# Adjacency words turned by a DMA instead of packed on TensorE, and VectorE's sorted rows begun three chunks later in layer 1

## The reference

```
h = relu(layernorm(x));  Wh = h @ W
e = Wh @ a[:256] + (Wh @ a[256:]).T          # layer 0: no nonlinearity on e
x = x + leaky_relu(softmax(where(adj, e, -1e9)) @ Wh, 0.2)
h = relu(layernorm(x))
e = leaky_relu(h @ a1[:256] + (h @ a1[256:]).T, 0.01)
x = x + softmax(where(adj, e, -9e15)) @ h    # layer 1
```

## Time and profile before

| | us |
|---|---|
| runs | 1846.00, 1840.76, 1846.56 |
| profiled execution | 1844.22 |
| its span | 1842.1 |
| PE busy | 1701.4 (92%) |
| DVE busy | 1224.0 (66%) |
| ACT busy | 940.5 (51%) |
| POOL busy | 650.3 (35%) |
| layer 0, first to last aggregate after the start | 155.12 to 1139.8 |
| POOL orders the lists | 901.45 to 1096.2 |
| first layer 1 gather to the last's start | 1148.59 to 1815.58 |

### The profile page before, as it was taken

One profiled execution on the slowest core, in us unless ns is written; L12 is line 12 of the kernel. 1 busy time (PEld: TensorE's weight loads), 2 busy tenths in 40 slices (PEclk: granted clock), 3 DMA queues, 4 the chain that ended last, 5 costly groups with the idle time before them and its releaser, 6 DMA issues. The chain is left out here.

```text
span 1842.1 us, 46596 instructions
## 1 busy us (share of the span) xinstructions
PE 1701.4 (92%) x17795; PEld 1460.9 (79%) x17795; DVE 1224.0 (66%) x4738; ACT 940.5 (51%) x1303; POOL 650.3 (35%) x607
## 2 busy tenths in 40 slices
PE   6889999999999999999999997677689999899887
PEld 5648888888888888888888886555578888788776
DVE  6577887888888888875533333677655655555655
ACT  5976554644565555546555541755444444444432
POOL 0000000000000000000255540888877777777775
PEclk9999999999999999999999999888989999999999
DMA  8409877978887797879999981644544444354442
GB/s 301 163 27 383 306 258 272 336 278 298 306 302 274 297 337 270 299 286 357 325 355 361 359 272 53 163 129 134 152 108 128 112 133 107 107 140 112 124 111 86
DMA packets 144110, 410.88 MB, mean 223 GB/s; under 512 B 26193, under 2 KB 92626, under 8 KB 111186
## 3 DMA queue, kind: packets, MB, share of 16 engines
q1 hardware_dynamic: 109714, 329.85, 49.8%
q0 software_dynamic: 27904, 73.43, 14.3%
q10 hardware_dynamic: 6336, 5.77, 1.1%
HBM read 368.94 MB, written 40.03 MB: 222 GB/s over the span
## 5 line engine op out<-in xcount | busy, mean ns | idle before, releaser
L956 PE MATMUL banks<-HV,adjT 128*128 128x257 f16 x8192 | 938.0, 273 | 5.6 <-DVE HV L656 5.2
L956 PEld LDWEIGHTS banks<-HV,adjT 128*128 128x128 fp8e4 x8192 | 788.7, 97 | 138.7 <-DVE HV L656 22.3
L1609 PE MATMUL banks<-Vp,adjp 128*128 128x257 f16 x2560 | 502.3, 278 | 92.7 <-DVE Vn L1409 53.4
L1235 POOL DMA_INDIRECT gat<-h_of_layer,rec x420 | 479.6, 1142 | 127.8 <-issue 125.7
L1609 PE MATMUL banks<-Vn,adjn 128*128 128x257 f16 x2560 | 501.4, 278 | 0.0
L428 ACT ACTIVATE adj_f<-adj_i 128x2048 fp8e4<-128x2048 int32 x256 | 474.1, 1897 | 6.8 <-DMA adj_i<-in_adj 4.5
L1609 PEld LDWEIGHTS banks<-Vp,adjp 128*128 128x128 fp8e4 x2560 | 249.9, 99 | 142.2 <-DVE Vn L1409 57.1
L409 POOL DMA_DIRECT2D HV<-x_after_layer x44 | 25.6, 581 | 849.6 <-DVE rank L879 796.6
L1609 PEld LDWEIGHTS banks<-Vn,adjn 128*128 128x128 fp8e4 x2560 | 252.6, 99 | 41.6
L1271 ACT ACTIVATE adjn<-h1bc,nh 128x512 fp8e5<-128x512 f32 x320 | 208.5, 711 | 104.0 <-PE banks L1609 93.4
L493 ACT ACTIVATE std<-mv,eps 128x1 f32<-128x1 f32 x64 | 18.8, 294 | 306.8 <-DVE mv L688 306.7
(11 more groups left out here) (157 smaller groups left out, 1455.5 us busy)
## 6 DMA issues: line engine op xcount, KB each, us to landing
adj_i<-in_adj SPq DMA_DIRECT2D x256, 1024.0 KB, 7.8
h_of_layer<-hh SPq DMA_DIRECT2D x64, 129.0 KB, 6.0
hs<-h_of_layer SPq DMA_DIRECT2D x64, 129.0 KB, 2.6
xt<-in_x SPq DMA_DIRECT2D x64, 128.0 KB, 6.1
packed_adj<-pk SPq DMA_DIRECT2D x64, 128.0 KB, 6.4
x_after_layer<-x SPq DMA_DIRECT2D x64, 128.0 KB, 6.0
HV<-in_x SPq DMA_DIRECT2D x7, 1024.0 KB, 11.9
gat<-h_of_layer,rec POOLq DMA_INDIRECT x420
```

The lines of the kernel that those rows point to most:

```text
L956: last = nc.tensor.matmul(acc[b][:, 0:DV], adjT_h[:, b, jb, :], V0[:, jb, s, 0:DV], start=(jb == 0 and s == 0), stop=(jb == T - 1 and s == 1))
L1235: pool.indirect_dma_start(gat[:, k % NBUF, s - s0, :], None, h_d, bass.IndirectOffsetOnAxis(ap=rec[:, m, s:s + 1], axis=0))\
L1609: mm = nc.tensor.matmul(bank[2 * i + part][:, 0:DV], m[:, i * P:(i + 1) * P], V[:, j, s, 0:DV], start=(j == 0 and s == 0), stop=(j == T - ...
```

## The change

It has three parts.

**The words are made on DVE and turned by a DMA.** `pack`, its constant and its PSUM banks are gone, and DVE's cast with them. The words are now those of `fold` (made for all 64 tiles); `turn`, an instruction on ACT's queue, transposes the 128x512 words in four 128x128 blocks into `pk` and signals `word_in`. `unpack` on DVE waits for that. Since the folded words pair other columns than the packed ones, tile and row numbers are permuted: a pair of tiles holds rows two apart (`x_v`, `adj_v`, `out_v`), `place` gives the bit and byte of a block, and PE's weights are read from `adjT` with a stride of two bytes, in layer 1 too.

**The steps are ordered anew.** ACT converts tile t+3 in step t (before: t+2) and turns t+2 at its end. DVE does fold part 0 of t+2, extract of t+1, unpack of t+1, decode, finish of t-1 with the other folds of t+2. `decode_bits` moves from the last of four steps to the third. SP's order is not touched.

**Layer 1.** Unpack is four operations of 128x512 for two chunks instead of eight of 128x256. With HEAD = 3.0, `rows_by` becomes 0, 0, 0, 0, 5, 12, 19, 26, 33, 40 and still ends at 420 after chunk 79.

The core of the diff:

```diff
+    def place(t):
+
+        k, q = divmod(t // 2, BQ)
+        return q, (k & 1) * 4 + (k & 2) + k // 4, t % 2
...
-    x_v = x.rearrange("(t p) d -> p t d", p=P)
-    adj_v = adj.rearrange("(t p) n -> t p n", p=P)
-    out_v = out.rearrange("(t p) d -> p t d", p=P)
+    x_v = x.rearrange("(m p h) d -> p m h d", p=P, h=2)
+    adj_v = adj.rearrange("(m p h) n -> m h p n", p=P, h=2)
+    out_v = out.rearrange("(m p h) d -> p m h d", p=P, h=2)
...
+                def turn(t, b, pb, reuse):
+
+                    act.wait_ge(fold_ready, t * 3 + 3)
+                    if reuse is not None:
+                        act.wait_ge(pk_out[pb], reuse)
+                    act.sem_inc(quarters_seen, 1)
+                    act.dma_start_transpose(pk[:, pb, :].rearrange("p (q r) -> p q r", q=BQ),
+                                            fold1[:, b, 1, :].bitcast(u16)).then_inc(word_in[pb], 16)
...
+                def step(t, j, reuse, pk_reuse, converts=True, turns=True):
+
+                    if converts:
+                        convert(t + 3, (j + 1) % 2, range(0, Q // 2), False)
+                    copy_sums(t - 1, (j - 1) % 2)
+                    if converts:
+                        convert(t + 3, (j + 1) % 2, range(Q // 2, Q), False)
+                    if reuse is not None:
+                        act.wait_ge(hh_out[(j - 1) % NX], reuse)
+                    finish(t - 1, (j - 1) % NX)
+                    if turns:
+                        turn(t + 2, j % 2, (j + 2) % NPK, pk_reuse)
```

```diff
-                    sp.wait_ge(pk_ready, t + 1)
-                    sp.dma_start(pk_d[bass.ds(t + off, 1), :, :].rearrange("o p n -> p (o n)"),
-                                 pk[:, pb, :]).then_inc(pk_out[pb], 16)
+                    sp.wait_ge(word_in[pb], 16 * (t // NPK + 1))
+                    sp.dma_start(pk_d[t + off, :, :], pk[:, pb, :]).then_inc(pk_out[pb], 16)
...
+                def unpack(t, b, pb, n_in):
+
+                    dve.wait_ge(word_in[pb], n_in)
+                    for i in range(HALF):
+                        if i <= 6:
+                            last = nc.vector.tensor_scalar(adjT[:, b, i, :], pk[:, pb, :], PAIR << i, 6 - i,
+                                                           ALU.bitwise_and, ALU.logical_shift_left)
                         else:
-                            i = nc.vector.tensor_scalar(dst, words, PAIR << k, k - 6, ALU.bitwise_and,
-                                                        ALU.logical_shift_right)
-                    i.then_inc(adjT_ready, 1)
+                            last = nc.vector.tensor_scalar(adjT[:, b, i, :], pk[:, pb, :], PAIR << i, i - 6,
+                                                           ALU.bitwise_and, ALU.logical_shift_right)
+                    last.then_inc(adjT_ready, 1)
...
-                def step(t, j, pk_reuse, n_in, x1_reuse, kept, off, ahead=True, lists=False, taken=False, e=None):
-
-                    if n_in is not None:
-                        normalise(t - 1, (j - 1) % 2)
+                def step(t, j, n_in, x1_reuse, kept, off, word_n, ahead=True, folds=True, listed=False,
+                         taken=False, e=None):
+
+                    normalise(t - 1, (j - 1) % 2)
+                    if folds:
+                        fold(t + 2, j % 2, 0)
+                    if taken:
+                        extract(t + 1, (j + 1) % UN)
                     if ahead:
-                        take_packed(t + 1, (j + 1) % 2, (j + 1) % NPK, pk_reuse, lists)
-                    if taken:
-                        extract(t, j % UN)
+                        unpack(t + 1, (j + 1) % 2, (j + 1) % NPK, word_n)
                     if e is not None:
-                        decode(e, (j + 1) % UN)
-                    if n_in is not None:
-                        finish(t - 1, (j - 1) % NX, n_in, x1_reuse, kept, off,
-                               (t + 1, (j + 1) % 2) if lists else None)
+                        decode(e, (j + 2) % UN)
+                    finish(t - 1, (j - 1) % NX, n_in, x1_reuse, kept, off,
+                           (t + 2, j % 2) if folds else None, listed)
...
-                        pack(k * 2 + b + 1, (b + 1) % 2, False)
                         aggregate(k * 2 + b, b)
```

```diff
-                            last = nc.tensor.matmul(acc[b][:, 0:DV], adjT_h[:, b, jb, :],
+                            q, i, h = place(jb)
+                            last = nc.tensor.matmul(acc[b][:, 0:DV], adjT_h[:, b, i, q, :, h],
...
+        HEAD = 3.0
...
-        pace = [FIRST * min(n, NC) + max(0, n - NC) for n in range(C)]
+        pace = [max(0.0, FIRST * min(n, NC) + max(0, n - NC) - HEAD) for n in range(C)]
...
-                    words = pkg[:, c // (NC // 2), :, :].rearrange("p g (t w) -> p t g w", w=WPB)
-                    for k in range(HALF):
-                        dst = adjp[:, c // UB % 2, :, :].rearrange("p t (g i) -> p t g i", g=G)\
-                            [:, :, :, k * WPB:(k + 1) * WPB]
-                        src = words[:, c % (NC // 2) * CB:(c % (NC // 2) + UB) * CB, :, :]
-                        if k <= 6:
-                            i = nc.vector.tensor_scalar(dst, src, PAIR << k, 6 - k, ALU.bitwise_and,
-                                                        ALU.logical_shift_left)
+                    q = c * CB // BITS % (BQ // 2)
+                    words = pkg[:, c // (NC // 2), :, q * P:(q + 1) * P]
+                    for k in range(UB * CB // 2):
+                        i = c * CB % BITS // 2 + k
+                        dst = adjp[:, c // UB % 2, k, :].rearrange("p (g r) -> p g r", g=G)
+                        if i <= 6:
+                            made = nc.vector.tensor_scalar(dst, words, PAIR << i, 6 - i, ALU.bitwise_and,
+                                                           ALU.logical_shift_left)
```

More of the change, by code:

```diff
@@ L634, in _ @@
                 for t in range(T - TAKE, T - TAKE + XC - 2):
                     take_wh(t)
-                    if t in UNPACKS:
-                        take_packed(UNPACKS[t], UNPACKS[t], UNPACKS[t], None)
+                    if t in FOLDS:
+                        for part in range(4):
+                            fold(FOLDS[t], FOLDS[t], part)
                 scales(NCH - 1)
@@ L646, in _ @@
                 nc.vector.memset(fl[:, :], 0.0)
+                unpack(0, 0, 0, 16)
+                unpack(1, 1, 1, 16)
                 dve.wait_ge(M_ready, 1)
@@ L699, in finish @@
                         fold(*folds, 3)
-                        fold(*folds, 4)
+                    if listed:
+                        make_keys(*folds)
                     dve.wait_ge(hh_ready, t + 1)
@@ L882, in _ @@
                 dve.wait_ge(v0_ready, T)
-                dve.wait_ge(const_in, 16 * 6)
+                dve.wait_ge(const_in, 16 * 5)
                 for t in range(2):
-                    fold(t, t, 0)
-                for t in range(2):
-                    for part in range(1, 5):
-                        fold(t, t, part)
-                    if t == 0:
-                        extract(0, 0)
+                    make_keys(t, t)
+                    extract(t, t)
+                for part in range(4):
+                    fold(2, 0, part)
+                make_keys(2, 0)
                 dve.wait_ge(hh_ones, 1)
                 for t in range(1, 2 * UN):
-                    step(t, t % UN, *counts(t), lists=True, taken=True,
-                         e=(t + 1) // UN - 1 if t >= UN - 1 else None)
+                    step(t, t % UN, *counts(t), listed=True, taken=True, e=(t - 2) // UN if t >= 2 else None)
                 with dve.Fori(2, NS // UN - 1) as k:
@@ L897, in _ @@
                 for t in range(NS - UN, T):
-                    step(t, t % UN, *counts(t), ahead=t + 1 < T, lists=t + 1 < NS,
-                         taken=t < NS, e=(t + 1) // UN - 1 if t < NS + UN - 1 else None)
+                    step(t, t % UN, *counts(t), ahead=t + 1 < T, folds=t + 2 < T, listed=t + 2 < NS,
+                         taken=t + 1 < NS, e=(t - 2) // UN if t < NS + 2 else None)
                     if t == SORT:
@@ L913, in _ @@
                 pe.wait_ge(ucol_ready, 2)
-                def pack(t, b, first):
-                    if not first:
-                        pe.wait_ge(pk_ready, t - 1)
-                    for q in range(Q):
-                        pe.wait_ge(conv_done, t * Q + q + 1)
-                        pe.sem_inc(quarters_due, 1)
-                        for jb in range(q * QB, (q + 1) * QB):
-                            last = nc.tensor.matmul(pkps[b][:, jb * WPB:(jb + 1) * WPB],
-                                                    adj_f[:, b, jb * P:(jb + 1) * P], packw[:, :],
-                                                    start=True, stop=True)
-                    last.then_inc(pack_done, 1)
                 def transpose_h(t):
```

193 lines of the change are left out of this document (79 added, 114 removed).

## The result

Four runs after took 2154.4 to 2160.07 us, median 2158.81, beside 1846.28 before on the same chip: ratio 1.169, 95% interval 1.167 to 1.172. The profiled execution's span is 2152.1 us. I had forecast 1838 in a range of 1785 to 1895; the change costs 312 us.

The account below looks back on a forecast made before the run. PE bounds layer 0 now and POOL's gathers layer 1; after the change the load chain would decide. 1844.2 − 5 (load chain) + 6 (transposing DMA) − 13 (ordering and dense stretch) + 4 (start) + 2 (layer 1) = 1838 us, range 1785 to 1895.

Parts of the forecast that it names:

- The transposing DMA: Between fold and unpack: words land in 5.7 us (2.6 to 6.8) against 5.4 available; +6 us, +30 at 6.8.
- rival B: Transposing DMA is late or takes the loads' bandwidth: 1893 us at 6.8 us landing, nearly 1920 at 8; chance 0.24.
- The load chain: SP's loads behind x1, sorted tiles: 63.1 us per four steps against 63.5 before; −5 us, between −23 and +26.
- my most likely error: The 3.5 us of start and tail in every load link; 1 us less would give −22 us.
- DVE's 55.9 us for four steps against PE's 57.2: Sorted steps: DVE alone would not bind, with 1.3 us of slack in 57.
- 358 that the late stretch moved: Load chain's slow case, in GB/s: 65.9 us per four steps, +26 us.
- its own rule: Landing time beyond 5.4 us counts in about two steps of four: 0.3 us over 10.75 rounds gives +6 us.
- Pack: Tiles 2 to 63 lose 1.6 us of PE each, 99 us, if PE stays the slowest.
- Strided weights: PE's 8192 loads reading every second byte cost nothing, with four times of room.
- Layer 1: Sum of shorter gathers from the new unpack, −8 us, and POOL's idle time, +10: +2 us.
- no slack to win it back: Layer 1: POOL idles before its 25th gather, +10 us (9 to 13), and cannot recover it.
- My −8 for the new unpack: Layer 1: four wide unpack operations instead of eight slow POOL's gathers less; −8 us (−3 to −10).

Follow-up runs that it names:

- e3_plain: Changed kernel with the words copied untransposed by one plain DMA: 2065.14 us on a slower chip, where the kernel before took 1989.3.
- f1_chop: Changed kernel with the words copied untransposed by four plain DMAs of 128x128 words, 512 packets of 256 bytes: 2166.21 us, ratio 1.176.
- e1_gate: Changed kernel with SP's load of tile k waiting until tile k-2's words have landed: 2175.84 us on a slower chip (kernel before 1989.3).
- f2_order: Changed kernel with SP issuing the next tile's load only after ACT has issued the transposing DMA: 1966.47 us, ratio 1.068.
- e9_earlyonly: Changed kernel with all four fold parts first in DVE's step and the transposing DMA issued early, xt's place unchanged: 1944.01 us, ratio 1.054.
- e5_latex: Changed kernel with SP issuing xt of tile k-1 in the turn of tile k, nothing else: 1804.35 us, ratio 0.978.
- g1_swapkeys: Changed kernel with xt one tile later on SP's queue, DVE's finish ahead of decoding, and keys made after decoding: 1774.52 us, ratio 0.963.
- e7_head: Kernel before with HEAD = 3.0 in layer 1's pace and nothing else: 1840.64 us, ratio 0.998.
- e6_early: Changed kernel with xt one tile later, all fold parts first in DVE's step, and the transposing DMA issued early: 1838.23 us, ratio 0.997.

## Why the prediction was wrong

- **The transposing DMA.** This is the step that failed: "I take 5.7", with 6.8 as the upper end and 8 us the worst case in rival B. It takes 13.1. Both ends came from plain transfers of 128 rows of 1 KB (144 packets each on ACT's queue, from its 6336); the transposing DMA has 544. What decides is the number of packets (e3_plain against f1_chop) and whether a load was issued ahead of them (e1_gate, f2_order). I had even noted that DMA capacity was 81% busy, but counted bytes.
- **The load chain.** The mechanism was right, that SP stands at xt until x1 and the loads behind it. The term that I called my most likely error was right as well: from SP's xt to the landing of the last quarter are 15.8 us in the step shown (506.39, 522.16) and 14.6 to 16.8 in four steps of e9_earlyonly, for my 15.3. What the sum lacked is DVE's idle time ahead of rden at each turn of its loop. For e9_earlyonly, twice 27.8, twice 0.9 more of folds and 7.5 of decoding are 64.9 us for four steps, with the 5.6 of idle time 70.5, and 71.4 are measured (the folds: 1.4 us of them have come into the chain and the 0.5 counted before has gone). For the chain as forecast that makes an estimated 68.7 us for four steps, 17.2 a step where I had 15.8, so even with the words in time the kernel would have been slower than before. The same idle time was missing where I set DVE's 55.9 us for four steps against PE's 57.2: with 3.0 to 5.6 us more DVE is the slower one, at 59 to 61. (In "358 that the late stretch moved" the row has 355; that changes the 65.9 by some 0.2 us.)
- **The two together.** I added them, with one as a small excess over slack. But the wait for x1 also sets when the load starts, 0.9 us ahead of the transposing DMA, and so makes the 13 us. Layer 0 by steps: 1469 as changed; 1281 with the DMA first (f2_order); 1118 with xt moved (e5_latex); 1148 before. So 188 us are the meeting and 163 the wait for x1 itself, with 30 us of the pack's 99 left as gain. The split hangs on the order: by e9_earlyonly (1252), which also moves the folds, it is 217 and 134.
- **Rival B** was the right one, decisive from 5.4 us on as said; its price was taken from 6.8 and 8 us. By its own rule (0.6 × 10.75 for 0.3 us) 13.1 would have given some +170 us, against the 188 above. That they are near is luck: the rule counts two steps of four, and in the trace every step waits, 23 times for 6.7 us.
- **The Trainium skill's** "as fast as regular DMAs" (Advanced Engine Details and Errata, X-Bar Transpose) agrees for a transposing DMA alone, 2.5 us in e1_gate against 2.3 in the earlier trace rows. Beside a load the plain copy in one piece takes 8.3 us and the transposing one 13.1, but the plain copy in as many packets 13.3. The Trainium skill's 1309 ns (VectorE: DVE Perf Modes, The three transpose paths) for 128x128, an estimated 5.2 us for four, are above the 2.5 us measured.
- **Pack.** Right that PE had 1.6 us a tile to give and that nothing on PE needed it; but only g1_swapkeys turns some 60 of the 99 us into time (layer 0 ends at 1088.3 instead of 1148.0).
- **Strided weights.** Right: 14.47 us for 128 matmuls either way at full clock.
- **PE's clock** I left out: with idle time in each step it is granted at 0.88, and a tile's matmuls take 16.1 us. It costs nothing here, since PE waits for adjT 131.3 us in the same 500.
- **Layer 1.** Idle time 8.6 for my 10, but "no slack to win it back" was wrong: e7_head, with HEAD alone, isn't slower. The sum was +2 and the two profiled executions say −11, of which little is sure. My −8 for the new unpack isn't shown by any run: e7_head has the old one and the same 1116 ns.

What stays open: the time of a small transfer beside a large one as a formula, and whether the load's packets or the amount of load issued ahead makes 13.1, 10.8 and 7.2 us. What DVE waits for at the turn of its loop. Nor did I try whether another queue than ACT's shares otherwise.

## What to carry to other kernels

Before a DMA is put into a loop, count its packets and not only its bytes, and ask what is in flight when it is issued: the same 128 KB took 2.4 or 13.1 us by 2.3 us of difference in order. When a wait on a queue of issues is moved nearer to its need, follow what is released behind it all at once. And try the queue's order first: one transfer moved by one tile was worth 350 us here. One mean of one execution is no proof of a few per cent: set it beside executions of the same code.

## What was not expected of the hardware

- 128 KB in 544 small packets issued 0.9 us behind a 4 MB load: 13.1 us, landing with the load's last quarter; in 144 packets 8.3 us; alone 2.4 to 2.5. With the load in eight DMAs of 4 KB packets 10.8, in sixteen of 2 KB 7.2.
- A load issued 1.4 us after them does not slow them: 2.4 us in the median (f2_order).
- DMA engines 98% busy for 294 GB/s when the two kinds mix all the time, 86% for 306 when they meet less (e6_early, e5_latex).
- VectorE stood idle once in four steps where its loop begins anew, 3.0 us before the change and 5.6 us in the window shown of e9_earlyonly, without a releaser in the profile.
- POOL's mean gather differs between executions of the same layer 1: 1104 to 1133 ns.
